# A two-layer graph network block on one core: the steady part of every engine's program written out, in place of a loop over pairs of groups

## What is computed

```
h = relu(layernorm(x))
Wh = h @ W;  e = leaky(Wh@a1 [:,None] + Wh@a2 [None,:]);  masked softmax over neighbours
keep the 16 largest weights of a row;  x = x + elu(att @ Wh)
h = relu(layernorm(x));  y = h;  mask2 = adj + eye > 0
for l in range(3):
    s = leaky((y@wi)[:,None] + (y@wj)[None,:] + b);  attn = softmax(s, mask2)
    t = layernorm(y + attn @ y) * g1 + beta1
    y = layernorm(t + gelu(t @ W1[l] + b1) @ W2[l] + b2) * g2 + beta2
out = x + y
```

## Time and profile before

| what | value |
|---|---|
| median of three runs | 2912.39 us |
| profiled execution: time, span of its instructions | 2917.91 us, 2916.2 us |
| mean granted TensorE clock | 0.978 |
| busy: PE, ACT, DVE, POOL | 2758.3, 2328.4, 2289.0, 2080.9 us |
| matmuls | 17764 |
| read and written in HBM | 47.34 and 37.75 MB |

### The profile page before, as it was taken

How to read it: one execution, slowest core, us unless ns; L and a number is a source line. 1 busy time by engine, 2 the same in 40 slices (tenths; PEclk the granted TensorE clock), 3 DMA queues, 4 the chain that set the end, 5 groups by cost and what they waited for, 6 DMA issues and landing times.

```text
span 2916.2 us, 59363 instructions
## 1 busy us (share of the span) xinstructions
PE 2758.3 (95%) x17764; PEld 2462.7 (84%) x17764; DVE 2289.0 (78%) x7766; ACT 2328.4 (80%) x4806; POOL 2080.9 (71%) x2217
## 2 busy tenths in 40 slices
PE   5689999999999999999999999999999999999995
PEld 4578988888988888888888888888898888889884
DVE  6777888888878788788887878788888888887543
ACT  4577888888888788888887878788887888898763
POOL 0356777787777777777777777777777778777774
PEclk9789999999999999999999999999999999999997
DMA  5000011011101101110101111101110111110001
GB/s 177 24 26 27 28 32 34 16 26 34 34 27 34 29 14 34 35 33 27 34 9 34 34 29 32 35 8 34 34 34 27 34 21 24 32 25 18 10 12 15
DMA packets 96384, 89.33 MB, mean 31 GB/s; under 512 B 9120, under 2 KB 94368, under 8 KB 96032
## 3 DMA queue, kind: packets, MB, share of 16 engines
q1 hardware_dynamic: 79136, 68.32, 7.5%
q0 software_dynamic: 16896, 16.78, 4.4%
HBM read 47.34 MB, written 37.75 MB: 29 GB/s over the span
## 4 chain that ended last, share of the span: by engine, by line
PE 50%; DVE 19%; ACT 13%; issue 10%; POOL 6%; DMA 1%; DVEq 0%; ACTq 0%; POOLq 0%; SPq 0%
PE ps_mm L3043 7%; PE ps_mm L3045 7%; PE ps_mm L3044 7%; PE ps_ff L3066 6%; PE ps_ff L3068 6%; PE ps_ff L3067 6%; PE ps_ag L3101 3%; ACT A L1070 2%; DVE junk L2269 2%; PE ps_ht L3113 2%; ACT H L1084 2%; PE ps L3165 2%; ACT a_hi L1078 2%; DVE U L2223 2%; POOL a_lo L507 2%
## 5 line engine op out<-in xcount | busy, mean ns | idle before, releaser
L3066 PE MATMUL ps_ff<-w_hi,a_hi 128*128 128x256 f32 x3072 | 898.3, 292 | 17.0 <-POOL a_lo L507 9.7
L507 POOL TENSOR_TENSOR a_lo<-A,a_hi 128x512 fp32r<-128x512 f32 x384 | 522.6, 1361 | 527.3 <-ACT a_hi L1078 519.6
L3067 PE MATMUL ps_ff<-w_lo,a_hi 128*128 128x256 f32 x3072 | 859.0, 280 | 0.0
L3068 PE MATMUL ps_ff<-w_hi,a_lo 128*128 128x256 f32 x3072 | 858.2, 279 | 0.0
L1070 ACT ACTIVATE A<-ps_mm,b_col 128x512 f32<-128x512 f32 x768 | 518.1, 686 | 308.7 <-PE ps_ff L3068 171.7
L3043 PE MATMUL ps_mm<-ht_hi,w_hi 128*128 128x512 f32 x1536 | 629.0, 410 | 29.0 <-issue 24.1
L3066 PEld LDWEIGHTS ps_ff<-w_hi,a_hi 128*128 128x128 f32 x3072 | 582.4, 190 | 57.9 <-POOL a_lo L507 31.1
L3045 PE MATMUL ps_mm<-ht_lo,w_hi 128*128 128x512 f32 x1536 | 609.0, 396 | 0.0
L3044 PE MATMUL ps_mm<-ht_hi,w_lo 128*128 128x512 f32 x1536 | 606.9, 395 | 0.0
L3067 PEld LDWEIGHTS ps_ff<-w_lo,a_hi 128*128 128x128 f32 x3072 | 583.1, 190 | 13.3
L3068 PEld LDWEIGHTS ps_ff<-w_hi,a_lo 128*128 128x128 f32 x3072 | 582.7, 190 | 0.0
(11 more groups left out here) (120 smaller groups left out, 5349.7 us busy)
## 6 DMA issues: line engine op xcount, KB each, us to landing
xr<-in_x SPq DMA_DIRECT2D x32, 512.0 KB, 4.1
out<-x SPq DMA_DIRECT2D x32, 512.0 KB, 4.5
out<-H POOLq DMA_DIRECT2D x32, 512.0 KB, 6.1
mask_in<-mask_park SPq DMA_DIRECT2D x96, 128.0 KB, 3.6
adj_sb<-in_adj SPq DMA_DIRECT2D x32, 256.0 KB, 4.4
mask_park<-mask_out SPq DMA_DIRECT2D x32, 128.0 KB, 3.7
X<-in_L_gnn_W SPq DMA_DIRECT2D x3, 1024.0 KB, 5.3
H<-in_L_gnn_W SPq DMA_DIRECT2D x3, 1024.0 KB, 6.9
```

What stands on the lines that cost most here:

```text
L507: pool.tensor_tensor(a_lo[:, at], A[:, at], a_hi[:, at].bitcast(F32), ALU.subtract).then_inc(s["a_lo_gpsimd"], 1)
L3066: pe.matmul(out_g, a_hi[:, at, cols], w2_hi[:, l, m], start=first, stop=False, skip_group_check=True)
L3067: pe.matmul(out_g, a_hi[:, at, cols], w2_lo[:, l, m], start=False, stop=False, skip_group_check=True)
L3068: last = pe.matmul(out_g, a_lo[:, at, cols], w2_hi[:, l, m], start=False, stop=final, skip_group_check=True)
```

## The change

The loop of `schedule` becomes a Python loop, so that each engine's program has the 22 steady iterations one after the other, with plain numbers in place of `At`.

```
         def schedule(opening, iteration, closing, eng):
 
             opening()
-            with eng.Fori(0, (LAST_STEADY + 1 - FIRST_STEADY) // 2) as j:
-                iteration(At(j, 2, FIRST_STEADY))
-                iteration(At(j, 2, FIRST_STEADY + 1))
+            for i in range(FIRST_STEADY, LAST_STEADY + 1):
+                iteration(i)
             closing()
```

## The result

The changed kernel takes 2841.9 us (median of 4 runs, 2839.9 to 2843.3) against 2912.6 us before in the same comparison, a ratio of 0.9758, 95% interval 0.9741 to 0.9775. The gain is 70.6 us. I had forecast 43.5 us, and a range that ended at 2856 us. The direction was right, the size was not.

What follows compares the result with a forecast made beforehand. PE's matmul stream was taken to bound the steady part. Terms 1 and 2 made 37.5 us; the mean pace of branch-free groups raised the gain to 43.5 us, so 2912.4 - 43.5 = 2869 us, range 2856 to 2886 us.

Steps and rivals of the forecast that it cites:

- Term 1: PE's taken branch at the end of a loop pass: ten waits for issue, 24.1 us, all of which goes.
- term 2: PE's clock falling after a taken branch: without the gap no fall, so 13.4 us go.
- Term 3: Pace of PE's steady groups without branches: mean of six branch-free groups, 84.6 us, a gain of 43.5 us in all.
- Registers and holds: Register and sequencer rows lost per pass on all engines: gain nothing, at most PE's idle 0.7 us a group, 14 us.
- I cost them at nothing by themselves: Loop branches of ACT, DVE and POOL: covered by PE's work, no cost; at worst 6.6 us of waits for low parts.
- (a): Another engine is next: steady groups each take 85.3 us, a gain of 30 us, 2882 us; chance 0.24.
- (b): PE's pause at the branch only hid other waits, so nothing goes: 2911 us, no change; chance 0.03.
- (c): Straight code must be read: late instruction blocks cost PE 3.75 us each, at one a group 2951 us; chance 0.04.

Runs made afterwards that it cites:

- act_loop: The changed kernel with the loop kept on ScalarE (ACT) alone, the other engines straight: 2856.4 us, 14.5 us over the straight kernel.
- topk_holds: The changed kernel, straight on all engines, with three semaphore increments put back in VectorE's top-16 in each group: 2862.1 us.
- holds_ordered2: The changed kernel with three increments back in VectorE's top-16, plus GpSimd's colliding scaling waiting until the top-16 beside it is done: 2845.7 us.
- long_pass: The kernel before, all engines looping, but two passes of ten groups each and the last two groups straight: 2886.3 us.
- dve_long: The changed kernel with VectorE alone looping, in two passes of ten groups, its last two groups straight: 2884.4 us.

## Why the prediction was wrong in size

*Term 1 and term 2* were right. Together they were forecast at 37.5 us; the two traces, subtracted, have 38.7 us from PE's branches on, and PE's loop alone costs 39.6 us. The rows of the straight kernel show neither the waits nor a lower clock between 353 and 2522 us.

*Term 3 failed.* "Their mean, ... = 84.6, gives 1692 us": the six groups that I took as the nearest thing to the changed kernel were not near enough. Two of them (524.2 to 609.5 and 2345.3 to 2429.4 us) had VectorE in its loop when it did the top-16, with the fourth instruction at 1.39 us; the changed kernel runs these two in 82.9 and 83.2 us where they took 85.3 and 84.1. The other four belong to the opening and the closing, whose order differs from the steady one: the changed kernel takes 84.5 and 85.3 us for the two of the opening, as before, and 167.3 us for the two of the closing, 1.3 us less. So four of six said something of other code, and two of the loop. The pace of the steady order without a loop, 83.3 us, stood in no window of the trace.

*"Registers and holds ... it is nothing"* is the step at the root. It counted what they delay on PE, and bounded it by PE's idle time, "that remaining 0.7 us a group, 14 us in 20 groups, is the upper bound". Both halves were wrong. Three increments on VectorE, 0.2 us in all, decide a race against GpSimd, and VectorE as the loser pays 1.04 us: 20 us over 22 groups, with three increments and nothing else. And PE's idle time is no bound, since a wait shorter than the drawn length of a matmul is drawn as work: PE's busy time fell by 39 us where I forecast 13.

*"I cost them at nothing by themselves"*, of the branches of the others, failed too. "PE does not wait for ACT there, its work on hand covers them" is contradicted by the trace of before itself: 9.9 us are lost behind ScalarE's ten branches, and act_loop loses 9.5 us at the same places. VectorE's branches were indeed covered, by PE's own, and cost some 24 us for nine when PE does not branch. The 68 ns read from the earlier trace rows is only the branch's record; VectorE then waits 16.6 us for issue in ten waits. Both went in the change at once, so the sum lacks ScalarE's 10 us. The same step would have misled anyone who unrolled PE alone and got 7 us.

*A small reading.* The traces have fewer rows of sequencers lost in a pass than I counted from the programs (79 on PE, 90 on DVE, 72 on ACT, 65 on POOL, for 101, 92 and some 80). Nothing above hangs on it.

*The rivals.* (a), a pace of 85.3 us from another engine, did not come: the other engines are what got faster. (b) and (c) did not either. PE's matmuls have no wait for issue in the straight code, and there are fewer instruction reads than before, so the price that I put on late blocks was never paid. The case that came, that VectorE's chain was on the path through a wait too short to be listed, was not among them.

Of the 70.6 us, then, about 39 are PE's branches with the clock, 14 to 16 the collision (topk_holds, holds_ordered2), about 10 ScalarE's branches, and some 7 lie elsewhere, with the registers and holds of VectorE and GpSimd as the likely but not the shown cause. Two kernels bear this out at the other end: with PE's loop alone the time is 2881.5 us, with all loops and no collision 2892.5, so the other loops cost 11 us beside PE's. What remains open is the pause that makes VectorE lose several times in four groups of long_pass and dve_long, and why the clock falls after some branches and not after others.

## What to carry to other kernels

Before bounding a cost by the idle time of a dense matmul stream, compare the distance between starts at each wait with the usual one: 0.2 us lost there is drawn as busy. Look for an instruction of VectorE or GpSimd whose duration is not its usual one; if the same instruction has two durations, it may be in a race with the other engine; if PE waits behind it, one semaphore wait that sets the order is worth trying (here 19 us on the loop, for one line). A branch's own record says little of how long its engine stands still; look at the waits for issue behind it. When several engines pause at nearly the same place in a loop, take the pauses away together: PE's alone gave 7 us, all gave 70.6.

## What the runs showed of the hardware

A taken branch at the end of a pass makes PE stand still for 2.1 to 2.8 us; its own record of 3.5 us begins earlier, and the same branch falling through takes 83 ns. A taken one leaves VectorE idle for at most 1.9 us and ScalarE for at most 2.1. A VectorE instruction of 0.35 us took 1.39 us whenever a GpSimd instruction of 1.39 us had started 0.14 us before it, and 0.35 us when it had itself started 0.07 us before. In long_pass one that started 0.02 us before lost too, and took 1.47 us; the boundary lies between these two leads. Three semaphore increments, 0.2 us together, cost a straight kernel 20 us by that, and 3.8 us when the order was fixed.
